# A two-layer convolution kernel whose patches are turned by DMA in float16 halves instead of by TensorE

## What is computed

```python
# layer 0: 3x3 convolution with the signs of the weights times alpha
x = x + conv3x3(gn(x), sign(weight) * alpha)
# layer 1
h = einsum('oc,bchw->bohw', w_in, gn(x))            # 64 -> 256 channels
f = rfft2(patches_8x8(h)) * fft_filt                # per channel and frequency
h = irfft2(f)                                       # back to pixels
h = depthwise_conv3x3(h, w_dw)
g = gelu(h[:, :128]) * h[:, 128:]
x = x + einsum('oc,bchw->bohw', w_out, g)           # 128 -> 64 channels
```

## Time and profile before

| | |
|---|---|
| median of 3 runs | 5495.8 us (5493.56 to 5497.33) |
| the profiled execution | 5494.37 us |
| its span | 5492.5 us |
| TensorE busy | 5361.2 us, 98% |
| VectorE busy | 4650.6 us, 85% |
| GpSimd busy | 4638.5 us, 84% |
| ScalarE busy | 3768.3 us, 69% |
| mean granted TensorE clock | 0.997 |

### The profile page before, as it was taken

The page is one execution under the profiler, slowest core; times in us unless marked ns, Lnnn a source line. Parts: engine busy times, 40 slices in busy tenths (PEclk is TensorE's granted clock), DMA queues, the critical chain, the costliest instruction groups (busy, mean ns, idle before and its releaser), DMA issues.

```text
span 5492.5 us, 173205 instructions
## 1 busy us (share of the span) xinstructions
PE 5361.2 (98%) x75428; PEld 3473.4 (63%) x75428; DVE 4650.6 (85%) x5703; ACT 3768.3 (69%) x4866; POOL 4638.5 (84%) x2727
## 2 busy tenths in 40 slices
PE   5999999999999999999999999999999999999998
PEld 4666666666666666666666666666666666666665
DVE  6889888888888888888888888888889888888876
ACT  3767767676676766767666676676767767677676
POOL 3888888898888988889888888888888888888898
PEclk9999999999999999999999999999999999999999
DMA  2011010110101101011010100101011010110000
GB/s 101 18 49 42 36 42 29 52 39 36 53 22 49 39 37 54 19 52 39 36 52 24 54 32 36 55 36 42 32 49 39 36 42 32 49 42 19 22 21 29
DMA packets 43843, 217.50 MB, mean 40 GB/s; under 512 B 5366, under 2 KB 6104, under 8 KB 36952
## 3 DMA queue, kind: packets, MB, share of 16 engines
q1 hardware_dynamic: 43096, 206.42, 9.8%
HBM read 103.64 MB, written 102.76 MB: 38 GB/s over the span
## 4 chain that ended last, share of the span: by engine, by line
PE 89%; DVE 7%; issue 2%; POOL 0%; ACT 0%; DMA 0%; SPq 0%; DVEq 0%; POOLq 0%; ACTq 0%
PE PS L952 27%; PE PS L969 21%; PE PS L912 14%; PE PS L941 11%; PE PS L982 6%; PE PS L930 6%; PE PS L921 4%; DVE hf L690 3%; DVE v L697 2%; DVE bn L628 1%; DVE g L722 1%; DVE PS L713 0%; DVE PS L706 0%; POOL v_lo L357 0%; DMA alpha_sb<-in_alpha 0%
## 5 line engine op out<-in xcount | busy, mean ns | idle before, releaser
L357 POOL TENSOR_TENSOR v_lo<-v,v_hi 128x1024 f16<-128x1024 f32 (+1 forms) x1792 | 3352.5, 1895 | 499.0 <-ACT v_hi L487 499.0
L697 DVE TENSOR_TENSOR v<-PS,smul 128x1024 f32<-128x1024 f32 (+1 forms) x1792 | 1916.1, 1087 | 424.8 <-PE PS L952 226.6
L487 ACT ACTIVATE v_hi<-v 128x1024 f16<-128x1024 f32 (+1 forms) x1792 | 1652.3, 944 | 707.2 <-DVE v L697 553.2
L952 PE MATMUL PS<-hf,c_nodes 64*128 64x512 f32 (+1 forms) x7168 | 1696.2, 574 | 7.4 <-DVE v L697 3.7
L969 PEld LDWEIGHTS PS<-c_ext,v_hi 128*128 128x128 f16 x14336 | 1128.2, 97 | 477.2 <-issue 289.2
L969 PE MATMUL PS<-c_ext,v_hi 128*128 128x100 f16 (+2 forms) x14336 | 1256.1, 203 | 5.1 <-ACT gel L507 3.4
L969 PE MATMUL PS<-c_ext,v_lo 128*128 128x100 f16 (+2 forms) x14336 | 1247.8, 202 | 0.0
L969 PEld LDWEIGHTS PS<-c_ext,v_lo 128*128 128x128 f16 x14336 | 1116.5, 97 | 1.2
L690 DVE TENSOR_TENSOR hf<-PS,mult 128x1024 f32<-128x1024 f32 (+1 forms) x896 | 955.1, 1087 | 85.0 <-PE PS L941 64.3
L952 PEld LDWEIGHTS PS<-hf,c_nodes 64*128 64x128 f32 x7168 | 570.6, 185 | 474.0 <-issue 125.3
L912 PE MATMUL PS<-S_hi,csign 64*64 64x448 f16 (+2 forms) x8640 | 738.8, 338 | 9.4 <-POOL S_lo L346 9.4
(11 more groups left out here) (74 smaller groups left out, 6242.4 us busy)
## 6 DMA issues: line engine op xcount, KB each, us to landing
out_x<-Xa SPq DMA_DIRECT2D x96, 448.0 KB, 2.5
out_x<-Xb SPq DMA_DIRECT2D x96, 448.0 KB, 2.5
Xa<-in_x SPq DMA_DIRECT2D x8, 2240.0 KB, 9.0
Xb<-in_x SPq DMA_DIRECT2D x8, 2240.0 KB, 9.0
Xa<-in_x SPq DMA_DIRECT2D x8, 1792.0 KB, 7.1
Xb<-in_x SPq DMA_DIRECT2D x8, 1792.0 KB, 7.6
Xa<-in_x SPq DMA_DIRECT2D x8, 1344.0 KB, 5.7
Xb<-in_x SPq DMA_DIRECT2D x8, 1344.0 KB, 5.9
```

What stands on the lines that cost most here:

```text
L357: nc.gpsimd.tensor_tensor(v_lo[:, img, :, k0:k1, :], v32[:, V_BUF[kind(b, s)][img][grp], :, 0:k1 - k0, :], v_hi[:, img, :, k0:k1, :], ALU. ...
L487: nc.scalar.activation(v_hi[:, img, :, k0:k1, :], v32[:, V_BUF[kind(b, s)][img][grp], :, 0:k1 - k0, :], ACT.Copy).then_inc(act_vhi[img], 1)
L697: nc.vector.tensor_tensor(v32[:, V_BUF[kind(b, s)][img][grp], :, 0:k1 - k0, :], PS[:, bank:bank + 2, 0:(k1 - k0) * C2].rearrange("p i (k c ...
L952: last = nc.tensor.matmul(PS[:, bank + side, 0:(k1 - k0) * C2], c_nodes[half, :], hf[half, img, k0:k1, :].rearrange("p k c -> p (k c)"), s ...
```

## The change

The identity matrix, `transposed`, `pixels` and the PSUM space of the transposes go. After `normalise_patches` ScalarE makes a float16 high part of the patches (`patches_high`), VectorE subtracts it for the low part (`patches_low`, both inputs in SBUF), and ScalarE's queue issues two DMA transposes from SBUF to SBUF (`turned`), one per part, of 128 x 896 float16 each. The forward transform is four float16 products per block, over all 128 pixels at once with a block-diagonal basis in high and low part, 28 per strip and 128 columns each. The spectrum `xf` now lies in the memory of `xn`, so normalising the next strip waits for the spectrum's low part. `n32` keeps one strip in place of two.

The front of a strip is shifted: `normalise_patches`, `patches_high`, `patches_low` and `turned` of strip t+1 stand in step t, the forward transform of strip t in step t. The sequences of all four compute engines and the order of the groups are written anew.

```diff
+            def patches_high(n, s, any_before):
+                i = n * STRIPS + s
+                act.wait_ge(act_xn, i + 1)
+                if any_before:
+                    act.wait_ge(dma_xT, 32 * i)
+                nc.scalar.activation(xn_hi[:], xn[:].rearrange("p q r c -> p (q r c)"), ACT.Copy).then_inc(act_xnh, 1)
+            def turned(n, s, any_before):
+                i = n * STRIPS + s
+                act.wait_ge(dve_xnl, i + 1)
+                if any_before:
+                    act.wait_ge(pe_xf, i)
+                nc.scalar.dma_start_transpose(xT_hi[:], xn_hi[:]).then_inc(dma_xT, 16)
+                nc.scalar.dma_start_transpose(xT_lo[:], xn_lo[:]).then_inc(dma_xT, 16)
+            def patches_low(n, s):
+                dve.wait_ge(act_xnh, n * STRIPS + s + 1)
+                nc.vector.tensor_tensor(xn_lo[:], xn[:].rearrange("p q r c -> p (q r c)"), xn_hi[:], ALU.subtract).then_inc(dve_xnl, 1)
...
-            def transposed(n, s, bank):
-                pe.wait_ge(act_xn, n * STRIPS + s + 1)
+            def forward_transform(n, s, bank):
+                pe.wait_ge(dma_xT, 32 * (n * STRIPS + s + 1))
                 for k in range(NBLK):
-                    last = nc.tensor.transpose(flat(bank, NBLK * 128)[:, k * 128:(k + 1) * 128],
-                                               xn[:, 2 * k:2 * k + 2].rearrange("p q r c -> p (q r c)"), c_id[:])
-                last.then_inc(pe_xT, 1)
-
-            def forward_transform(n, s, bank):
-                pe.wait_ge(act_xT, n * STRIPS + s + 1)
-                for k in range(NBLK):
-                    for side in range(2):
-                        half = slice(side * P * P, (side + 1) * P * P)
-                        last = nc.tensor.matmul(PS[:, bank + side, k * P * P:(k + 1) * P * P], xT[half, k, :], c_fwd[half, :],
-                                                start=True, stop=True)
+                    for part, (xT, fwd) in enumerate(((xT_hi, fwd_hi), (xT_lo, fwd_hi), (xT_hi, fwd_lo), (xT_lo, fwd_lo))):
+                        last = nc.tensor.matmul(flat(bank, NBLK * BPX)[:, k * BPX:(k + 1) * BPX], xT[:, k, :], fwd[:],
+                                                start=part == 0, stop=part == 3)
                 last.then_inc(pe_xf, 1)
```

More of the change, by code:

```diff
@@ L247, in build @@
         pe_out = sem("pe_out")
-        N_CONST = 15
+        N_CONST = 14
         N_CONV = 4
@@ L293, in _ @@
                 sp.dma_start(alpha_sb[r * C:(r + 1) * C], alpha).then_inc(dma_conv, 16)
-            for dst, src in ((c_fwd[:], forward), (c_pick, pick), (c_pair[:], pair), (c_apart[:], apart), (c_id[:], identity),
+            for dst, src in ((fwd32, forward), (c_pick, pick), (c_pair[:], pair), (c_apart[:], apart),
                              (c_nodes[:], nodes), (c_taps, taps), (ext32, ext), (filt_sb, filt), (wdw_sb, w_dw),
@@ L373, in image @@
                             low_strip(n + 1, NORM_STEPS[t][0])
+                        if mid:
+                            low_nodes(mid[0], mid[1], 0, 0)
+                        if more and len(NORM_STEPS.get(t, ())) > 1:
+                            low_strip(n + 1, NORM_STEPS[t][1])
+                        if mid:
+                            low_nodes(mid[0], mid[1], 0, 3)
                         if done:
@@ L572, in image @@
                         if mid:
-                            high_nodes(mid[0], mid[1], 0, 3)
-                        if done:
-                            lifted(done[0], done[1], 1)
-                        if front:
-                            pixels(n, t, BANK_P)
+                            high_nodes(mid[0], mid[1], 0, 2)
+                        if more and len(NORM_STEPS.get(t, ())) > 0:
+                            strip32(n + 1, 1 - par, NORM_STEPS[t][0], False)
                         if up:
@@ L753, in image @@
                                 dve.wait_ge(pool_vlo[1], 4 * i)
-                            weighted(b, s, 0, 0, BANK_P)
-                            if before and conv_before:
-                                dve.wait_ge(pool_vlo[1], 4 * i - 2)
-                            elif before:
-                                dve.wait_ge(pool_vlo[1], 4 * i - 2)
-                            weighted(b, s, 0, 1, BANK_Q)
-                        if up:
-                            gated(up[0], up[1], 0)
@@ L827, in image @@
                             dve.wait_ge(pool_vlo[0], 4 * i + 1)
-                            weighted(b, s, 0, 0, BANK_P)
+                            weighted(b, s, 0, 2, BANK_P)
+                        if up:
+                            gated(up[0], up[1], 0)
+                        if more:
+                            convolved(n + 1, 1 - par, conv_strips(t)[0], BANK_Q)
+                            stats_1(n + 1, 1 - par, conv_strips(t)[0])
+                            convolved(n + 1, 1 - par, conv_strips(t)[1], BANK_P)
+                            stats_1(n + 1, 1 - par, conv_strips(t)[1])
                         if up:
@@ L877, in _ @@
             shift_1(0)
+            patches_low(0, 0)
             image(0, 0, False, True, True)
@@ L1003, in image @@
                     if more and CONV_FROM <= t <= CONV_TO:
+                        if mid:
+                            if conv_before and before:
+                                pe.wait_ge(dve_v[1], 4 * i - 1)
+                            elif before:
+                                pe.wait_ge(dve_v[1], 4 * i - 1)
+                            widened(b, s, 3, BANK_Q)
                         if done:
```

434 lines of the change are left out of this document (210 added, 224 removed).

## The result

The changed kernel took 6079.8 us (median; 6065.3 to 6106.2) beside 5495.6 us for the kernel before on the same chip: a ratio of 1.107, 95% interval 1.105 to 1.109. The forecast was 5447 us, its range ended at 5690.

A forecast was written before the change was run, and what follows sets the result against it. TensorE was taken to set the pace, VectorE level with it in plain steps after the change. From 5494.4 us: -42 over fifteen pairs, -10 for the last plain steps, +3 at the start; median 5447 us, range 5310 to 5690.

The forecast's parts named there:

- What it takes from TensorE: TensorE: transposes gone, 0.82 us shorter, new transform 0.02 longer; 0.8 us per strip, 180 us if nothing takes its place.
- rival E: TensorE's transform: weight loads not hidden, 1.1 us more per strip, 166 us more in all, 5613 us; chance 0.03.
- The issue: ScalarE's queue, ahead of lifted: two DMA transpose issues at 0.66 us together, half of it charged in convolution steps.
- Rival B: ScalarE's queue ahead of lifted: issues at 2.4 us a pair, convolution steps 1.74 longer, 178 us more, 5625 us; chance 0.22.
- The wait on the port shared with GpSimd: VectorE's new subtraction waits for GpSimd's running instruction: 0.5 us taken in plain steps, bounds 0 and 1.46.
- Rival C: Shared port in plain steps: the wait is 1.46 us in place of 0.5, 101 us more, 5548 us; chance 0.12.
- GpSimd's side: GpSimd losing 1.09 us a strip to the subtraction, plain steps 18.5 to 19.6 us; by the skill, shown by no row.
- Landing: The two 224 KB transfers, ahead of the next step's transform: 5 us taken, at least 8 available, so hidden.
- D: Landing late: 16 us for the pair, transform 8 us late in every step, about 7200 us; chance 0.06.
- the convolution's bank: Convolution steps: the bank now waits for the weighted group evaluated right ahead of it; some 0.2 us more per step.
- The full gain (A): Whole kernel: no shared-port wait and issues hidden, so all 180 us are gained, 5316 us; chance 0.10.

The follow-up runs named there:

- e3: Changed kernel with its transposes issued by SyncE and two bn_stats in place of patches_low (low part zero): 5499.4 us, ratio 1.0008 to the kernel before.
- e1: Changed kernel with its two DMA transposes issued from SyncE's queue in place of ScalarE's: 5752.3 us, ratio 1.047 to the kernel before.
- e2: Changed kernel with patches_low replaced by two bn_stats with one SBUF input (low part zero): 5788.3 us, ratio 1.053 to the kernel before.
- e7: e3 without any instruction in patches_low's place, SyncE waiting for the high part alone (low part zero): 5481.5 us, ratio 0.9974 to the kernel before.
- e4: Kernel before plus two one-block DMA transposes per step at the end of ScalarE's sequence, into unread scratch tiles: 5610.8 us, ratio 1.021.
- e6: Changed kernel with one DMA transpose of 14 blocks in place of two of 7, still in ScalarE's queue: 5854.4 us, ratio 1.065.
- e8: Changed kernel with one 14-block transpose issued by SyncE and patches_low one place earlier in convolution steps: 5559.7 us, ratio 1.012.

## Why the prediction was wrong, by its own steps

- **What it takes from TensorE: right, 0.75 us for 0.80.** From the transform's start to the next group's it is 1.57 us beside a convolution, for 1.54 forecast, and 1.67 in plain steps, where it was 1.51 before in both (the new records, 56 ns apart, end 1.74 us after the start for 1.70). The transposes held TensorE 0.82 us beside a convolution and 0.91 in plain steps. But its busy time fell only from 5361 to 5222 us in e3, where nothing slows the clock: 139 us, for 180 in the forecast. The evaluated groups hold TensorE 0.33 us longer in each plain step of the new sequences (7.43 us for 7.10) and 0.09 beside a convolution; why, wasn't looked into. The load of 98 ns is hidden; rival E falls. By the Trainium skill (TensorE: Matmul & The Clock Gate, section Back-to-back issue gap), with 81 ns for each product, the 28 would have taken an estimated 2.27 us; the trace doesn't agree.
- **The issue: the step that failed.** "I take the near end, 0.66 for the two", half of it charged. They took 2.6, in series with `lifted`, which TensorE waits for. Rival B named mechanism and place, and its size for a step was right too: it made convolution steps 1.74 us longer, and e1 gives back 1.65 in those at the full clock. Taking the issues off ScalarE gave 327 us, more than B's 178: 110 of it is busy time of TensorE (5373 to 5263 us) as its mean clock went from 0.973 to 0.994 (below), and the step behind the convolutions gave 2.2 us per pair.
- **The wait on the port shared with GpSimd: a second step that failed, by place.** Taken 0.5 us in plain steps, bounds 0 to 1.46, and nothing beside a convolution. Measured 1.2 in the mean, 1.95 beside a convolution, 0.5 to 0.8 in plain steps. The bound of 1.46 was one wait of one line, not a limit: `v_lo` lasts 2.13, and whoever comes just behind its start waits nearly all of it. Rival C had the mechanism but charged plain steps; it was the convolution steps that paid.
- **The sum over rivals: they were treated as exclusive.** The causes named in B and C were both there, in series through one instruction, since the issue waits for the subtraction. Their prices add (327 and 292 us, 580 together), and the range, which ended at B alone, missed it.
- **GpSimd's side.** The prediction left it out of the sum, since no row showed it. It is there: GpSimd's busy time rose by 176 us, 0.8 in each strip.
- **Landing: right that it is hidden**, at 2.6 us for the 5 taken; D falls.
- **A step was left out:** the step behind the last convolution costs 6.4 us more. Its `patches_low` takes 2.69, and its `lifted` stands ahead of the group statistics on TensorE, which waits.
- **The clock.** In several convolution steps the granted clock has spells at its lower level (1.2 GHz): its mean over the step is 0.90 or 0.95 of full, and TensorE's busy time rises from 26.7 to 28.2 or 29.5 us. In the step behind them it is 0.88. Before, it was 1.00 in every window cut. What TensorE did ahead of that: it idled twice for about 1.7 us in each of these steps. Not every such step has a spell: 1843.74:1874.40 idled as long and kept 1.00. With one of the two causes gone the mean over the span is 0.994 (e1) or 0.986 (e2), with both 0.997 (e3). By these rows idle time of TensorE cost more than its own length; that the idling brings the spells is argued from their order and from e1 to e3, where both shrank together, and no run tests it alone.
- **The sum without the two costs was too good as well.** In e3 a pair lasts 337.6 us as before: six convolution steps 27.1 each for 27.3 (forecast 27.0), the step that normalises 26.95 for 28.4 (forecast: no change), the step behind the convolutions 22.4 for 20.9, the six other plain ones 125.7 for 124.7 (forecast: one less). Beside a convolution the prediction's 0.2 for the convolution's bank was right (0.26 measured); the 0.33 that the projection waits for `gated` was not in it. The full gain (A) wasn't there to be had in either set of sequences that was tried. The prediction saw VectorE and TensorE level in plain steps, and took the sum of VectorE's work for the bound; e7 took that work away and the step stayed. What holds it is the order in which a bank or a buffer is handed round, and only the chain of waits shows that.

## What to carry to other kernels

A DMA issue is an instruction of the queue that holds it: price it by its own kind, count what stands behind it, and put it on a queue that nobody waits for (here worth 327 us), or make two issues one (225 us). Here an instruction that needed what another engine was using cost up to the whole rest of that engine's running instruction, so its place against the other queue mattered more than its length: moving one line gave back 192 us. And work taken from the busiest engine is a gain only as far as the next loop through the other engines allows; with three engines at 84% and more, look for that loop in the chain of waits before charging the saving in full.

## What the runs showed of the hardware

- The issue of a DMA transpose from SBUF to SBUF cost 1.11 us for one 128x128 block of float16, 1.24 for seven and 1.49 for fourteen in ScalarE's queue, 1.23 for seven and 1.48 for fourteen in SyncE's (medians; e4, the changed kernel, e6, e1, e8); a plain store's 0.33. It landed after 2.4, 2.6 and 3.4 us.
- A VectorE instruction with two SBUF inputs and a GpSimd `tensor_tensor` held each other back for what was left of the running one: a subtraction of 1.09 us took 3.04 behind a `v_lo` of 2.13, and a `v_lo` that came behind it took 2.97. VectorE's `bn_stats` with one SBUF input was held by nothing (0.63 us at most, e2).
- TensorE's 28 products of 128x128 by 128 columns in float16, each with its own weights, follow each other every 56 ns, with weight loads of 98 ns beside them.
